# Moving a count matmul and a half-precision split in an eight-turn fused loop

## What is computed

```python
h = concat([patch_conv(x, W, b)[hilbert order], txt], axis=1)      # (32, 333, 192)
q = layernorm(h)
dw = depthwise_conv(q, dw_w, 9 taps); pw = grouped(dw, pw_w) + pw_b
kern = grouped(pw * q, ak_w) + ak_b                                # 12 heads x 9 taps
w = softmax(kern); v = q @ pt_w.T + pt_b
h = h + sum_k w[..., k] * v[token + k - 4]
x2 = layernorm(h); scores, idx = top_k(x2 @ Wg, 2); weights = softmax(scores)
pos = cumsum(onehot(idx)) - 1; keep = pos < capacity
h = h + sum over kept (token, expert): weight * ((a * silu(b)) @ W2[e]),  a, b = split(x2 @ W1[e])
```

## Time and profile before

| what | value |
|---|---|
| time, median of 3 runs | 1508.36 us (1505.85 to 1512.7) |
| profiled execution | 1510.98 us |
| its span, first to last instruction | 1509.2 us |
| first stage | to about 810 us |
| TensorE, VectorE, ScalarE, GpSimd busy | 83%, 66%, 30%, 48% |

### The profile page before, as it was taken

The page is one execution under the profiler, slowest core; times in us unless marked ns, Lnnn a source line. Parts: engine busy times, 40 slices in busy tenths (PEclk is TensorE's granted clock), DMA queues, the critical chain, the costliest instruction groups (busy, mean ns, idle before and its releaser), DMA issues. The chain is left out here.

```text
span 1509.2 us, 23369 instructions
## 1 busy us (share of the span) xinstructions
PE 1253.0 (83%) x8476; PEld 999.6 (66%) x8476; DVE 998.9 (66%) x1924; ACT 449.8 (30%) x949; POOL 719.4 (48%) x545
## 2 busy tenths in 40 slices
PE   6969898888978888861651799999998999999994
PEld 6757676666757666550431577877877787787883
DVE  4208959889898989999662365656564565656552
ACT  2011222323212232311121344434342433434331
POOL 1000311656555555756556355464455345545445
PEclk9989999999998899885675899999999999999997
DMA  9895463565655253544112546473646455554533
GB/s 317 321 349 153 116 193 69 147 163 155 166 151 161 90 163 87 142 108 124 41 46 90 121 60 102 69 106 50 111 56 105 54 88 79 64 102 61 72 44 37
DMA packets 224280, 178.54 MB, mean 118 GB/s; under 512 B 128872, under 2 KB 208006, under 8 KB 224160
## 3 DMA queue, kind: packets, MB, share of 16 engines
q1 hardware_dynamic: 176896, 117.16, 31.9%
q0 software_dynamic: 37248, 36.15, 15.8%
q10 hardware_dynamic: 10016, 23.66, 4.3%
HBM read 69.22 MB, written 89.23 MB: 105 GB/s over the span
## 5 line engine op out<-in xcount | busy, mean ns | idle before, releaser
L1121 POOL DMA_INDIRECT out<-yb,meta x200 | 329.5, 1648 | 325.7 <-DVE yb L1178 254.7
L1210 DVE TENSOR_TENSOR hidden<-silu,bankU 128x320 f32<-128x320 f32 x320 | 155.1, 487 | 199.5 <-PE bankU L1243 167.9
L894 PE MATMUL bankK<-normedT,conv_w 128*128 128x333 f32 x864 | 267.4, 456 | 0.0
L85 POOL DMA_INDIRECT expert_inputs<-slot_rows,slots x176 | 225.7, 1282 | 79.8 <-issue 56.4
L1150 ACT ACTIVATE silu<-bankG 128x320 f32<-128x320 f32 x320 | 139.9, 437 | 383.5 <-PE bankG L1243 348.1
L894 PEld LDWEIGHTS bankK<-normedT,conv_w 128*128 128x128 f32 x864 | 163.1, 194 | 73.7 <-issue 5.2
L1256 PE MATMUL bankY<-w_high,hidden_high 128*128 128x192 f16 x800 | 196.8, 246 | 0.0
L1258 PE MATMUL bankY<-w_high,hidden_low 128*128 128x192 f16 x800 | 196.8, 246 | 0.0
L1257 PE MATMUL bankY<-w_low,hidden_high 128*128 128x192 f16 x800 | 196.8, 246 | 0.0
L650 DVE TENSOR_TENSOR prod<-window_values,kb 128x960 f32<-128x960 f32 (+1 forms) x135 | 174.5, 1302 | 3.6
L668 DVE TENSOR_TENSOR hidden_group<-hidden_group,prod 128x960 f32<-128x960 f32 (+1 forms) x135 | 175.9, 1303 | 0.3
(11 more groups left out here) (131 smaller groups left out, 2209.5 us busy)
## 6 DMA issues: line engine op xcount, KB each, us to landing
patches<-in_x SPq DMA_DIRECT2D x16, 1536.0 KB, 8.2
token_rows<-rowbuf SPq DMA_DIRECT2D x32, 492.0 KB
expert_inputs<-prod ACTq DMA_DIRECT2D x8, 1470.0 KB, 15.4
window_values<-token_rows SPq DMA_DIRECT2D x32, 264.0 KB
hidden_group<-token_rows SPq DMA_DIRECT2D x32, 264.0 KB
expert_inputs<-prod ACTq DMA_DIRECT2D x8, 980.0 KB, 17.2
window_values<-token_rows SPq DMA_DIRECT2D x32, 192.0 KB
kb<-token_rows SPq DMA_DIRECT2D x32, 148.5 KB
```

What stands on the lines that cost most here:

```text
L85: nc.gpsimd.indirect_dma_start(out=xslots[:, :], out_offset=bass.IndirectOffsetOnAxis(ap=idx[g % 2][:, k, r:r + 1], axis=0), in_=xrow[g % ...
L894: mm = T_.matmul(bankK[(u + t) % 2][:, 0:L], conv_w[:, t // 2, k, :], qT[u][:, t, k:k + L], start=(k == 0), stop=(k == K - 1))
L1121: nc.gpsimd.indirect_dma_start(out=out[:, :], out_offset=bass.IndirectOffsetOnAxis(ap=meta[t % NMETA][:, c, 0:1], axis=0), in_=yb[v][:, c, ...
L1210: V.tensor_tensor(hf[j % 2][:, m * HALF:(m + 1) * HALF], sg[m][:, :], bankU[m][:, 0:HALF], ALU.mult).then_inc(prod_done, 1)
```

## The change

Two things are moved; nothing is added or left out.

First, `counts_before(h)` stands behind both halves of `patch(p + 3)` on TensorE and not between them. VectorE's two reads of the counts bank, with the `pre_read` that frees it, are taken out of `places` into a function `offsets`, which stands ahead of `places`, and so ahead of the wait for ScalarE's exponential and the three operations that follow it. One window operation is moved from ahead of the pair to behind it: `part(3)` becomes `part(2)`, and the last part of the turn grows by one. At the end of the stage `offsets` stands directly ahead of `places`.

Second, GpSimd's `low_parts` of slice 0 of a group stand in the next turn, behind `pair_norm(2 it + 1)` and ahead of the scatter, and no longer at the end of their own turn. The last of them, for group 6, stays where it was.

```diff
@@ block.gpsimd
                 for it in range(NG):
                     pair_norm(2 * it + 1)
+                    if it > 1:
+                        low_parts(it - 2, 0)
                     if it > 2:
                         scatter(it - 3, 0)
...
                     if it:
                         slice_norm(it - 1, 0)
-                        low_parts(it - 1, 0)
+                low_parts(NG - 2, 0)
                 scatter(NG - 3, 0)
@@ block.vector
+                def offsets(g):
+
+                    dve.wait_ge(pre_ready, g + 1)
+                    done(V.tensor_tensor(off[:, :], bankN[:, CN:CN + 16], base[:, :], ALU.add))
+                    a = done(V.tensor_tensor(base[:, :], base[:, :], bankN[:, CN + 16:CN + 32], ALU.add))
+                    after(a)
+                    dve.sem_inc(pre_read, 1)
+
                 def places(g):
...
                     done(V.tensor_tensor(w12[:, 1, :], w12[:, 0, :], ex[:, :], ALU.mult))
-                    dve.wait_ge(pre_ready, g + 1)
-                    done(V.tensor_tensor(off[:, :], bankN[:, CN:CN + 16], base[:, :], ALU.add))
-                    a = done(V.tensor_tensor(base[:, :], base[:, :], bankN[:, CN + 16:CN + 32], ALU.add))
-                    after(a)
-                    dve.sem_inc(pre_read, 1)
...
                     if it > 1:
                         top_two(h)
-                    part(3)
+                    part(2)
                     if it > 1:
+                        offsets(h)
                         places(h)
-                    part(6 if it > 1 else 12)
+                    part(7 if it > 1 else 13)
@@ block.tensor
                     if p + 3 < NPAIR:
-                        patch(p + 3, (0,))
+                        patch(p + 3)
                     if it > 1:
                         counts_before(h)
-                    if p + 3 < NPAIR:
-                        patch(p + 3, (1,))
                     for c in range(3):
                         scores(p + 1, c)
```

More of the change, by code:

```diff
@@ L858, in _ @@
                 top_two(g)
+                offsets(g)
                 places(g)
@@ L863, in _, with patch @@
                 T_ = nc.tensor
-                def patch(p, tiles=(0, 1)):
+                def patch(p):
                     u = p % 2
                     pe.wait_ge(x_loaded[u], 16 * (p // 2 + 1))
-                    for c in tiles:
+                    for c in range(2):
                         wait(pe, h_in_rows, 2 * p + c - 1)
```

## The result

The changed kernel takes 1482.15 us (median of 4 runs, 1478.12 to 1483.34) where the kernel before, timed beside it, takes 1507.11: ratio 0.9824, 95% interval 0.9806 to 0.9843. That is 25 us less. The forecast was 1488.9, 19.5 us less, so the direction and the place are right and the size is a quarter too small: on the 1508.36 us of the table ahead of the prediction the ratio gives 26.5 us less, 1481.8, just past the end of the range (1482 to 1500).

The account below looks back on a forecast made before the run. VectorE, nearly the bound, waits for the convolution bank through GpSimd's low parts and pair_norm. Low parts 17.8 us plus earlier read at the stage's end 1.7 give 19.5 us off 1508.4: 1488.9 us, range 1482 to 1500.

Parts of the forecast that it names:

- the count's move in the turns: Counts behind the whole patch start scores 4.4 us earlier, but bring 0 in it=3 to 6, with bounds 0 to 3.8.
- What bounds it: First stage: VectorE nearly the bound, waiting 16.7 us for the convolution bank behind GpSimd's low parts and pair_norm.
- The low parts' 17.8 us: Low parts of slice 0 behind pair_norm start normalising 4.3 to 4.6 us earlier in it=3 to 6: 17.8 us.
- the chain keeps the bound and the whole 4.6 counts: In it=6 the bank comes 24.0 us after normalising starts; VectorE still waits 0.8 us, so all 4.6 us are gained.
- the rival "more": Less TensorE idle ahead of the transposes keeps the clock at 2.4 GHz: 25 us gained, 1483 us; chance 0.12.
- its 4.91 us stay about as long: TensorE's idle time ahead of the transposes stays near 4.91 us, or shrinks where values wait for VectorE.
- Contention 0: Moved low parts beside softmax_top's passes over kb cost VectorE -0.5 to +1.2 us a turn; taken as 0.
- 1.7 at the end: In it=7 the counts bank is read 1.7 us earlier, taking 1.7 us off the end of the first stage.
- Only one half does anything alone: Moving the low parts by themselves brings 15.9 us; moving the count by itself is worth 1.7 us.
- The slower rival: Low clock lasts through scores and convolutions, ending 13.3 us late; four turns give +53 us, 1561 us; chance 0.05.
- "no change": Low clock for the whole patch makes VectorE wait 2.7 us in offsets in five turns: 1502 us; chance 0.13.
- The signs: Right: bank waits about 3 us, normalising 4.3 to 4.6 earlier, load waits gone; wrong: offsets waits, slow kb passes.

Follow-up runs that it names:

- the fills: The kernel before with 17, then 24 idle matmuls ahead of the transposes in it=3 to 6: 1508.42 us, ratio 0.9995, then 1504.90 us, ratio 0.9969.
- the low parts further back: The changed kernel with GpSimd's low parts of slice 0 moved behind seven scatters and slice 1's rstd: 1476.17 us, ratio 0.9790.
- the late read: The changed kernel with VectorE's read of the counts bank put back inside places, behind the third piece of window work: 1493.88 us, ratio 0.9892.
- the order alone: The kernel before with only the count matmul moved behind the whole patch, its bank read where it was: 1511.56 us, ratio 1.0016.

## Why the prediction was right or wrong

**The step that failed** is the price of the count's move in the turns: "on their own they are worth nothing in it=3 to 6", and with it "I therefore give the count move 0 here". Measured, the count's half brings 11 us by itself and 21 us when the low parts are moved as well, and without it the low parts bring 5.7 and not the 15.9 to 17.8 us that were priced for them.

**What bounds it: right.** The chain aggregates, low parts, pair_norm, normalising, bank is what was waited for. pair_norm starts 0.08 us behind the aggregates, and the bank waits fell from 16.7 to 1.4 us (forecast about 3). Normalising starts 4.95, 4.81, 3.96 and 4.01 us earlier behind the aggregates in it=3 to 6, 17.7 us in all, so the subtraction of 17.8 is right for the start of normalising.

**The low parts' 17.8 us as time: right only beside the count's move.** The step to "the chain keeps the bound and the whole 4.6 counts" took 24.0 us from normalising to the attend as fixed. In the changed kernel the bank is ready at 529.79 + 5.26 = 535.05, 22.0 us behind 513.05. That is the rival "more", with its cause as told: less idle ahead of the transposes (0.59 us, not 4.91), patch at 2.4 GHz. Here "its 4.91 us stay about as long" failed. The wait is normalising's start less TensorE's arrival, and the change makes the first 4.0 us earlier behind the aggregates in this turn; TensorE arrives earlier only by what scores gain, and part of this went into a convolution at the low clock (6.64 us). In the kernel before, the fills show that the clock in this stretch is worth about 5 us by itself.

**Contention 0: mis-sized.** The bound was -0.5 to +1.2 us a turn, and "I take 0" was the wrong end. The subtraction went from 1.40 to 2.60, and the low parts further back brought 5 us, left out 7. The clue was in the earlier trace rows; I used it for the add only, and forgot that the subtraction has two inputs as well.

**The count's move at 0 (0 to 3.8) and 1.7 at the end: wrong, and the largest error.** It treated the scores' arm as a side arm that ends in VectorE's loads. With the low parts moved, that arm ends in TensorE's transposes too, by ScalarE's queue, and with the late read and no low parts of slice 1 the turn shown above is TensorE's. The prediction also left out that the scores set when GpSimd's low parts of slice 1 run, and so what they run beside: by itself the count's half shows as 4.7 us less busy time of VectorE in the turns and 3.8 us in the last turn, where the 1.7 of the read was right and 1.9 of shorter low parts was missing. That the busy time is the cause of the gain in the turns is argued for the count alone, not tested; with the low parts moved as well it was tested, and is not. The read, which I had put at 1.7 us once, is worth 10 to 13.

**Only one half does anything alone: false, both ways.** The low parts alone brought 5 to 6 us, not 15.9, the count alone 11, not 1.7.

**Why the sum still came near.** This was luck: two errors cancelled. The gain of the low parts was priced as if nothing else stood close behind, and what stands close behind was removed by the very part that I had priced at nothing. The slower rival and "no change" did not come: no wait of VectorE in offsets shows in its list of waits.

**The signs.** Of those for "right", the bank waits, pair_norm's start and the scores (3.4 us behind the counts, forecast 3.5) came; normalising came 4.0 to 4.95 us earlier (forecast 4.3 to 4.6), and the load waits are not gone but 1.5 us. Of those for "wrong", a kb pass of 2 us or more came, the subtraction.

**What stays open.** Why the order alone costs 2 us without the low parts moved (its five turns, 422.8 us, and its last turn, 53.0, are no longer than before), and how the 10 us that belong to both halves divide between TensorE's turn and VectorE's busy time: there is one trace for each kernel, and the traced execution lies up to 9 us from the median. What the late read costs in the turns, lateness or clock, is open too.

## What to carry to other kernels

When two chains of nearly equal length end in one place, price them together: neither half of a change need be worth its own subtraction until both are moved, and then they can be worth more than the sum, as here (26.5 us against 5.7 and 10.9). Follow a late result through every engine's queue behind the one that waits for it, since a copy that stands behind an unrelated exponential ties two chains. Where two engines lengthen each other, ask which instruction the moved work will lie beside, and put it beside work that keeps its length.

## What the runs showed of the hardware

A GpSimd subtraction of two SBUF inputs and a VectorE instruction with two SBUF inputs lengthen each other. Where both started at 509.2, the GpSimd pair took 4.1 us and VectorE's three window instructions 5.1, against 2.2 and 3.4 apart. VectorE's kb subtraction, which overlapped the low parts of slice 0 for 1.3 us, took 2.60 and not 1.40. VectorE's reduce (1.39) and statistics (1.66) kept their length beside the same GpSimd work.

With 14 idle matmuls around the counts the scores ran at the high clock, and then a convolution was 1.2 to 1.4 us slower in two turns and a patch 1.6 to 1.9 us slower in two others; the total was the same. With 24 idle matmuls ahead of the transposes of the kernel before, the patch behind them took 8.01 us in all four turns and not 9.01 to 9.91, and the kernel was 5 us faster. So what idle matmuls bring depended on what stood behind the wait that they filled.
